# Keys of the third attention block: projected in the quantised stage before it, kept in device memory, loaded per step

## What is computed

```python
def bitlinear(x, w, b):
    xq = act_quant(rmsnorm(x))
    wq = weight_quant(w)
    return jnp.einsum('bsd,fd->bsf', xq, wq) + b
...
x = x + tanh(g_ffn[1]) * bitlinear(gelu(bitlinear(LN(x), w1, b1)), w2, b2)       # layer 1, quantised
# layer 2, masked attention; queries = LN(x), keys = values = context, 16 heads of 8
q = queries @ Wq + bq
k = keys @ Wk + bk
v = values @ Wv + bv
attn = softmax(where(masks, q k^T / sqrt(8), -1e9))
x = x + tanh(g_xattn[2]) * (rearranged(attn v) @ Wo + bo)
```

## Time and profile before

| | |
|---|---|
| median of 3 runs | 2562.04 us (2560.22 to 2562.13) |
| the profiled execution | 2556.09 us, of which its span is 2554.3 us |
| PE, DVE, ACT, POOL busy over the span | 85%, 71%, 53%, 48% |
| `l1` alone with its queue of steps | about 920 to 1190 us of the span |
| quantised stage alone | about 1190 to 1374 us |
| `l2` with its router | about 1374 to 1770 us |

### The profile page before, as it was taken

One profiled execution on the slowest core, in us unless ns is written; L12 is line 12 of the kernel. 1 busy time (PEld: TensorE's weight loads), 2 busy tenths in 40 slices (PEclk: granted clock), 3 DMA queues, 4 the chain that ended last, 5 costly groups with the idle time before them and its releaser, 6 DMA issues. The chain is left out here.

```text
span 2554.3 us, 78270 instructions
## 1 busy us (share of the span) xinstructions
PE 2168.7 (85%) x32243; PEld 1663.2 (65%) x32243; DVE 1823.6 (71%) x5057; ACT 1356.6 (53%) x2507; POOL 1213.6 (48%) x1728
## 2 busy tenths in 40 slices
PE   6999999999987959997555999993999688787597
PEld 5887887878864747775443677772566457666375
DVE  4777777777773658888985688986455388999454
ACT  3555555555542338787995555550222177788232
POOL 1334434344344531116773145556566666887444
PEclk9999999999998979998876999995999866888599
DMA  6320000000006621110000011112555322332363
GB/s 199 112 110 27 27 24 27 22 22 20 19 18 182 174 63 54 58 50 7 1 1 20 27 45 54 52 44 79 155 160 161 91 79 60 98 94 71 94 187 102
DMA packets 213955, 184.50 MB, mean 72 GB/s; under 512 B 33420, under 2 KB 189654, under 8 KB 213600
## 3 DMA queue, kind: packets, MB, share of 16 engines
q1 hardware_dynamic: 194144, 142.52, 19.2%
q0 software_dynamic: 19456, 36.99, 4.2%
HBM read 102.01 MB, written 72.68 MB: 68 GB/s over the span
## 5 line engine op out<-in xcount | busy, mean ns | idle before, releaser
L614 POOL DMA_INDIRECT slots<-row,put x256 | 258.6, 1010 | 193.1 <-issue 129.7
L1941 PE MATMUL experts_H<-experts_xs_t,experts_w 128*128 128x512 f32 x576 | 265.6, 605 | 6.9 <-DMA experts_b<-in_F_b 2.6
L1097 ACT ACTIVATE l_prob_t<-l_banks 128x512 f32<-128x512 f32 x256 | 132.2, 602 | 146.1 <-PE l_banks L1214 116.5
L1467 POOL TENSOR_TENSOR l_var_eps<-l_mv,eps 128x1 f32<-128x1 f32 x64 | 12.2, 191 | 413.9 <-DVE l_mv L1548 413.9
L1959 PE MATMUL experts_Y<-experts_w,experts_hid 128*128 128x128 f32 x1664 | 197.8, 275 | 3.5 <-DVE experts_y L1889 2.6
L1806 POOL DMA_INDIRECT rows<-experts_y,experts_idx x160 | 155.5, 972 | 91.4 <-DVE experts_y L1885 50.9
L1959 PEld LDWEIGHTS experts_Y<-experts_w,experts_hid 128*128 128x128 f32 x1664 | 191.7, 192 | 5.4 <-issue 5.4
L1503 DVE TENSOR_REDUCE l_top<-l_S 128x16 f32<-128x1024 f32 x64 | 78.3, 1224 | 160.4 <-PE l_S L1646 160.4
L1941 PEld LDWEIGHTS experts_H<-experts_xs_t,experts_w 128*128 128x128 f32 x576 | 106.1, 194 | 115.9 <-issue 107.2
L1008 DVE TENSOR_REDUCE l_top<-l_banks 128x32 f32<-128x2048 f32 x64 | 146.5, 2289 | 48.0 <-PE l_banks L1221 36.3
L912 POOL TENSOR_TENSOR l_var_eps<-l_mv,eps 128x2 f32<-128x2 f32 x96 | 24.1, 251 | 307.7 <-DVE l_mv L978 216.5
(11 more groups left out here) (312 smaller groups left out, 6041.3 us busy)
## 6 DMA issues: line engine op xcount, KB each, us to landing
experts_w<-in_F_w SPq DMA_DIRECT2D x104, 256.0 KB, 3.6
l_ctx_t<-in_ctx_t SPq DMA_DIRECT2D x96, 128.0 KB, 2.4
early_q_m<-l_q_t SPq DMA_DIRECT2D x384, 32.0 KB, 1.8
experts_xs<-slots SPq DMA_DIRECT2D x40, 264.0 KB, 2.9
slots<-l_empty SPq DMA_DIRECT2D x16, 536.0 KB, 4.0
experts_xs<-slots SPq DMA_DIRECT2D x16, 536.0 KB, 4.4
slots<-l_empty SPq DMA_DIRECT2D x16, 520.0 KB, 6.0
experts_xs<-slots SPq DMA_DIRECT2D x16, 520.0 KB, 4.4
```

The costliest lines, as they stand in the source:

```text
L614: pool.indirect_dma_start(self.slots, bass.IndirectOffsetOnAxis(ap=g.put[c][:, tile:tile + 1], axis=0), g.row[:, tile, self.sent_cols], No ...
L1097: nc.scalar.activation(prob_t[:, t.par(PROB), r, :], Z[:, r, :], ACT.Exp).then_inc(prob_done, 1)
L1941: nc.tensor.matmul(H[:, c, :], w1_s[:, t.par(2), c, :], xs_t[:, t.par(2), :], start=True, stop=True).then_inc(h_filled[c], 1)
```

## The change

The keys of `l2` for all 32 items are computed in the quantised stage, one item a step, from u = 9 to u = 40. For each, SP loads the context of the item into `ctx_t` of `l1` (step u-2 of it), TensorE does the product into a free PSUM bank, VectorE adds the bias and writes it to a slot of `k_t`, and SP stores the slot to `keys2` in device memory. The block now ends only when all stores have landed. In `l2` L1234 and L1101 are gone; SP loads the keys of an item one step before PROJ, and `k_m` is made from `k_t` in SBUF, without a bias, where it was made from PSUM. In the diff, the lines of `vector` stand between L2114 and L2123, those of `tensor` between XT and HT, SP's load of the keys behind the four DMAs of `q_m`; `l2` is called with `keys=g.keys`, the other two attentions without.

```diff
 class Quantised:
+    CTX_FIRST, KEYS_FIRST = 7, 9
...
+        self.KEYS = banks[:, 5, 0:256]
...
+    def key(self, u, first):
+        return u - first if 0 <= u - first < self.ITEMS else None
+
+    def sync(self, sp, u):
+        j = self.key(u, self.CTX_FIRST)
+        if j is not None:
+            wait(sp, self.keys_filled, j - 3)
+            sp.dma_start(self.ctx_t[:, j % 4, :], self.g.ctx_t[:, 256 * j:256 * j + 256]).then_inc(self.keys_ctx[j % 4], 16)
+        j = self.key(u, self.KEYS_FIRST)
+        if j is not None:
+            sp.wait_ge(self.keys_drained, j + 1)
+            sp.dma_start(self.g.keys[:, 256 * j:256 * j + 256], self.k_t[:, j % 4, :]).then_inc(self.keys_stored[j % 4], 16)
+        if u == self.STEPS - 1:
+            for k in range(4):
+                sp.wait_ge(self.keys_stored[k], 16 * self.ITEMS // 4)
...
 def vector(self, dve, u):
+        j = self.key(u, self.KEYS_FIRST)
+        if j is not None:
+            wait(dve, self.keys_filled, j + 1)
+            wait(dve, self.keys_stored[j % 4], 16 * (j // 4))
+            V.tensor_scalar(self.k_t[:, j % 4, :], self.KEYS, self.g.early.bk[1][:, :], None, ALU.add).then_inc(self.keys_drained, 1)
...
 def tensor(self, pe, u):
+        j = self.key(u, self.KEYS_FIRST)
+        if j is not None:
+            wait(pe, self.keys_ctx[j % 4], 16 * (j // 4 + 1))
+            wait(pe, self.keys_drained, j)
+            self.nc.tensor.matmul(self.KEYS, self.g.early.wk[1][:, :], self.ctx_t[:, j % 4, :], start=True, stop=True).then_inc(self.keys_filled, 1)
...
+                if keys is not None and t.live(3):
+                    slot = t.par(3, SLOTS_QK)
+                    wait(sp, p_filled, t.done(3 + SLOTS_QK))
+                    sp.dma_start(k_t[:, slot, :], keys[:, t.item(3) * 256:t.item(3) * 256 + 256]).then_inc(k_in[slot], 16)
...
-                    nc.scalar.activation(k_t[:, t.par(PROJ, SLOTS_QK), :], QK[:, 256:512], ACT.Identity, bias=bk_s[:, :])
+                    if keys is None:
+                        nc.scalar.activation(k_t[:, slot, :], QK[:, 256:512], ACT.Identity, bias=bk_s[:, :])
...
+                        if keys is not None:
+                            wait(act, k_in[slot], reused(t, PROJ, SLOTS_QK))
                         for j in range(4):
-                            last = nc.scalar.activation(k_m[:, t.par(PROJ, SLOTS_QK), j, :], QK[:, 256:512], ACT.Identity,
-                                                        bias=bk_masked[:, j:j + 1], scale=g.const[:, C_JMASK + j:C_JMASK + j + 1])
+                            src, bias = (QK[:, 256:512], bk_masked[:, j:j + 1]) if keys is None else (k_t[:, slot, :], 0.0)
+                            last = nc.scalar.activation(k_m[:, slot, j, :], src, ACT.Identity, bias=bias, scale=g.const[:, C_JMASK + j:C_JMASK + j + 1])
...
-                    nc.tensor.matmul(QK[:, 256:512], wk_s[:, :], ctx_t[:, t.par(PROJ, SLOTS_CTX), :], start=True, stop=True)
+                    if keys is None:
+                        nc.tensor.matmul(QK[:, 256:512], wk_s[:, :], ctx_t[:, t.par(PROJ, SLOTS_CTX), :], start=True, stop=True)
```

More of the change, by code:

```diff
@@ L773, in beats, with attention_split @@
     return max(0, min(t - first + 1, n))
-def attention_split(nc, g, name, gate_col, kind, head=None, stream=None, router=None, together=None, weights=None, out=None, follow=None):
+def attention_split(nc, g, name, gate_col, kind, head=None, stream=None, router=None, together=None, weights=None, out=None, follow=None, keys=None):
     ITEMS = TILES // 2
@@ L837, in attention_split @@
         own = len(ph.held)
-        follower = follow and follow(nc, ph, g, banks)
+        follower = follow and follow(nc, ph, g, banks, ctx_t, k_t)
+        k_in = keys is not None and [ph.sem(f"k_in{k}") for k in range(SLOTS_QK)]
         block = ctx.enter_context(nc.Block(no_gpsimd_drain=True))
@@ L891, in step @@
                     sp.dma_start(tokens(out, STREAM + 1, t), g.x[:, t.item(STREAM + 1) * 2:t.item(STREAM + 1) * 2 + 2, :]).then_inc(x_stored, 16)
-            for t in range(ITEMS + STREAM + 1):
+            for t in range(FOLLOW + follower.STEPS if follower else ITEMS + STREAM + 1):
                 if tail and t == 4:
                     tail.load(sp)
-                step(Step(sp, ITEMS, t))
+                if t < ITEMS + STREAM + 1:
+                    step(Step(sp, ITEMS, t))
+                if following(t):
+                    if t - FOLLOW == follower.CTX_FIRST:
+                        sp.wait_ge(xv_filled, XV_BEATS)
+                    follower.sync(sp, t - FOLLOW)
             if weigh:
@@ L1098, in step @@
                 if t.live(PROJ):
+                    slot = t.par(PROJ, SLOTS_QK)
                     wait(act, qk_filled, t.done(PROJ))
-                    nc.scalar.activation(k_t[:, t.par(PROJ, SLOTS_QK), :], QK[:, 256:512], ACT.Identity, bias=bk_s[:, :])
+                    if keys is None:
+                        nc.scalar.activation(k_t[:, slot, :], QK[:, 256:512], ACT.Identity, bias=bk_s[:, :])
                     last = nc.scalar.activation(q_t[:, t.par(PROJ, SLOTS_QK), :], QK[:, 0:256], ACT.Identity, bias=bq_scaled[:, :], scale=SCALE)
@@ L1342, in handed_over @@
                     pe.wait_ge(prob_done, 4 * ITEMS)
+                if u == follower.KEYS_FIRST:
+                    pe.wait_ge(xv_drained, XV_BEATS)
                 if u == follower.HT_FIRST:
@@ L1979, with __init__ @@
     STEPS = ITEMS + DEPTH - 1
-    XT_FIRST, H_FIRST, HT_FIRST, Y_FIRST = 5, 6, 10, 11
+    XT_FIRST, H_FIRST, HT_FIRST = 5, 6, 10
+    CTX_FIRST, KEYS_FIRST = 7, 9
     ROOTS, SCALES = ITEMS + 8 - 1, ITEMS + 8 - 3
-    def __init__(self, nc, ph, g, banks):
-        self.nc, self.g = nc, g
+    def __init__(self, nc, ph, g, banks, ctx_t, k_t):
+        self.nc, self.g, self.ctx_t, self.k_t = nc, g, ctx_t, k_t
+        self.keys_filled, self.keys_drained = ph.sems("keys_filled keys_drained")
+        self.keys_ctx, self.keys_stored = ([ph.sem(f"{n}{k}") for k in range(4)] for n in ("keys_ctx", "keys_stored"))
+        self.KEYS = banks[:, 5, 0:256]
         RING = self.RING
@@ L2232, in build @@
         g.slots = dram("slots2", EXPERTS * REGION, R_LOGITS - R_XN)
+        g.keys = dram("keys2", P, TOKENS)
         x0, rows2 = dram("x0", TOKENS, D), dram("rows2", 2 * TOKENS, D)
@@ L2239, in build @@
         attention_split(nc, g, "l1", 1, "softmax", stream=x0, follow=Quantised)
-        attention_split(nc, g, "l2", 2, "masked", router=(t["F2_wg"], None, "top2", g.slots), together=4, weights=6)
+        attention_split(nc, g, "l2", 2, "masked", router=(t["F2_wg"], None, "top2", g.slots), together=4, weights=6, keys=g.keys)
         experts(nc, g, "experts2", g.slots, rows2, t["F2_w1"], None, t["F2_w2"], None, "silu", 6)
```

## The result

The median goes from 2562.04 us (5 runs) to 2577.98 us (5 runs, 2567.11 to 2582.59): ratio 1.0062, 95% interval 1.0038 to 1.0087: slower, by 0.6%. The forecast was 2578. The profiled execution is the fastest of the five, 2567.11 us with a span of 2564.8, and the 10.5 us by which its span is longer than that of before have to be taken apart.

A forecast was written before the change was run, and what follows sets the result against it. In the quantised stage ScalarE was taken to bound at full clock, a ring of TensorE and VectorE waits at half clock. Profiled execution 2556.1 + 24 - 8 = 2572; the median, 6.0 higher, 2578 us; range 2556 to 2594.

The forecast's parts named there:

- The ring at half clock, ScalarE at full clock: Quantised stage: waits between TensorE and VectorE set the step at half clock (5.81 us), ScalarE at full clock (5.37 us).
- The quantised stage, +24: Keys' product and evacuation lengthen late turns by 1.17 us, 0.86 a step on the mean, 28 times: +24 us (-5 to +40).
- the count of late turns: Quantised stage: L2114 waits for Y in 19 of 26 steps, each taking all of the 1.17 us: 0.86 a step.
- The last three items and the transfers, nothing: Quantised stage: items u = 38 to 40 fit into L2114's 2.23 us wait, and loads and stores hold nothing up: 0 us.
- `l2`, -8: `l2` without L1234 saves 0.43 to 0.50 us of TensorE in each of 32 steps: -8 us, bounds 0 to -14.
- the waits of L667: `l2`, VectorE: where L667 waits, 10 times in 25 steps, L1280 comes 0.45 us earlier: 4.5 us gained, waits all but gone.
- what was named as the danger: `l2`: with less work TensorE could lose clock; half-clock time, costing 5 us today, if doubled takes 5 of the 8 back.
- the first six steps: `l2` up to 1436 us, clock 0.75: L1234 costs up to 0.84 us a step, half taken as gained: 2.6 us.
- Hidden by ScalarE: Rival, quantised stage: turns lengthen only under ScalarE's floor, step stays 5.56 us; -8, 2554 us; chance 0.09.
- half clock everywhere: Rival, quantised stage: every turn runs at half clock, +40 - 8, 2594 us; chance 0.16.
- `l2` without gain: Rival: `l2` gains nothing, since VectorE sets its steps or TensorE loses clock; +24, 2586 us; chance 0.10.
- The clock given back: Rival, quantised stage: busier TensorE gets 2.4 GHz and turns drop below 5.37 us; -5 - 8, 2549 us; chance 0.09.

The follow-up runs named there:

- after_filled: Changed kernel with four products that nobody reads added behind Y on TensorE in every full step; ratio to before 0.9959, median 2546.19 us.
- after_half_filled: Changed kernel with two products that nobody reads added behind Y on TensorE in every full step; ratio to before 0.9965, median 2545.86 us.
- transfers_only: Changed kernel without the keys' product and evacuation, storing the loaded context itself as keys, all transfers kept; ratio to before 0.9977, median 2551.31 us.
- The filled kernels: Three kernels with unread products behind Y: four on the kernel before, four or two on the changed one; ratios to before 0.9968, 0.9959, 0.9965.
- product_out: Changed kernel with the keys' product moved behind Y, the evacuation kept between L2155 and L2170, one step later; ratio to before 0.9992, median 2556.68 us.
- both_out: Changed kernel with the keys' product moved behind Y and the evacuation ahead of L2155, one step later; ratio to before 0.9977, median 2547.89 us.
- the two fills: Changed kernel with four, or with two, unread products behind Y in every full step; ratios to before 0.9959 and 0.9965.

## Why the prediction was right

That forecast and median, 2578 and 2577.98, agree this closely is luck: the five executions spread over 15 us, and the profiled one, which the sum put at 2572, took 2567.11. What was right are the path and the signs of the two terms; their sizes came out as follows.

*The ring at half clock, ScalarE at full clock: right.* The changed kernel lengthens the turn and not ScalarE's work, and ScalarE's idle time went from 4.9 to 30.2 us, above the 25 named. That full clock would hide the new work was an argument when it was written; after_filled and after_half_filled show it, 5.33 and 5.34 us.

*The quantised stage, +24: measured +27.0 (bounds -5 to +40).* The product was put at 0.84 us at half clock and took 0.85; the evacuation at 0.33 and took 0.39. The term was too small in the count of late turns: 19 of 26 were taken over from before, and 24 of 26 waited. Most late turns were cheaper than thought, 6.74 us (1231.79 - 1225.05) and not 6.98 (three took 7.35), since H still runs at 2.4 GHz in a turn like the one shown: 0.62 us, where the turn of before had 1.01; only XT, the product and HT behind it have 1.2. The two errors stand against each other: 1.04 us a step against 0.86. That count did not fit the step of before either: 19/26 x 5.81 + 7/26 x 5.37 = 5.69, where 5.56 had been measured, since a turn that is not late can take 4.98 us (1255.59 - 1250.61). The 26 full steps, 26 x 1.04, make up all of the +27.0: the stretch ahead of them, with the first items, took 0.4 us more than before, the one behind them 0.4 less.

*The last three items and the transfers, nothing: right.* From the last L2170 to the last L2176 it is 18.31 us, against 18.70 from L2123 to L2129. The last evacuation starts 5.2 us before that last L2176, and its store has landed by 1393.1. In transfers_only the same stretch takes 21.46 us, but not for its transfers: its last three HT take 1.97 us each, at 1.2 GHz, where the last two of before took 1.10 and 1.09.

*`l2`, -8: measured -8.0, and -7.1 over all kernels* (the mean of the eight with loaded keys is 320.0 us, of the four without 327.0). The step of the argument that put it at the waits of L667 was wrong: they are not all but gone, 4.1 us are left of 5.8. The gain is a whole product, 0.43 us, in each short step, and what was named as the danger, clock that is lost in `l2` as well, took a part back: the steady part went from 0.98 to 0.95. That the sum still came to 8 is luck too. The sixth queries' product of `l2`, before and after:

```profile
1428.26 0.59 PE L1235 MATMUL l_banks<-l_xn_t,early_wq 128*128 128x256 f32 x2
```

```profile
1444.97 0.67 PE L1251 MATMUL l_banks<-l_xn_t,early_wq 128*128 128x256 f32 x2
```

Up to it `l2` gained 54.85 - 48.83 = 6.0 us, where 2.6 had been put on the first six steps; behind it 273.65 - 271.65 = 2.0 us, where 4.5 + 0.8 had been put on the waits of L667 and L1035. Over all kernels, eight against four as above, the two parts are 3.8 and 3.3 us.

*The rivals.* Hidden by ScalarE, half clock everywhere and `l2` without gain fall by the rows above. The clock given back did not come, 0.73 after 0.75, and the reason named against it is borne out: the gap in which TensorE waits for VectorE stayed, and it grew from 58.9/26 = 2.3 us to 2.6. The Trainium skill (TensorE: Matmul & The Clock Gate, Part 1) has it that activity releases the throttle. The filled kernels agree with that, at 0.99 to 1.00; the changed kernel, with one product more in each step, stayed at 0.73, but its step grew with the work, and TensorE's busy share only went from 84.32/145 = 58% to 103.93/172 = 60%. The share alone does not tell the clock either: it is 66% in product_out at 0.79 and 66% in after_half_filled at 1.00. What went with the clock was where the work stands: both_out does the same work as the changed kernel at 0.88.

## What to carry to other kernels

Work that is added to an engine with idle time need not be free. Here it was free outside the ring of waits that sets the step, and inside it only once the ring, at full clock or opened, had become shorter than ScalarE's step: look for the wait that the engine ends its idle time with, and put the work into it, not ahead of it. Where a stage runs at both clock levels, price an added product at each, and look at whether the edit closes or stretches TensorE's gap, since the clock can be worth more than the work. A second place in PSUM that takes H's wait for its reading out altogether gave the lowest ratio here, 0.9940, with all of the change's other edits kept; the two fills gave 0.9959 and 0.9965, with intervals that overlap it.

## What the hardware showed that we had not expected

Two products of 128 x 256 f32 that nobody reads, 1.08 us in a step of 5.34, brought TensorE's clock from 0.73 to 1.00 and the whole kernel from 1.0062 to 0.9965 of before. H's wait became 0.8 us shorter by it; whether the shorter wait or the added work brought the clock up no run separates.

In `l2` the clock fell in steps in which TensorE hardly paused: 12.51 of 12.69 us busy at a clock of 0.73. What stands ahead of the slow part in that step of the changed kernel:

```profile
1494.12 2.05 PE L1287 MATMUL l_banks<-l_val,l_prob_t 128*64 128x18 f32 x64
1496.35 0.28 PE L1338 MATMUL l_banks<-early_bias_rows,const_bf 3*128 3x128 bf16 x2 [0.18 <-DVE l_top L1019]
1496.56 1.13 PE L1343 MATMUL l_banks<-early_wo,l_ctx_out 64*64 64x128 f32 x16
```

L1343 takes 1.13 us here and 0.67 in a step at full clock:

```profile
1560.80 0.28 PE L1338 MATMUL l_banks<-early_bias_rows,const_bf 3*128 3x128 bf16 x2 [0.19 <-DVE l_top L1019]
1561.02 0.67 PE L1343 MATMUL l_banks<-early_wo,l_ctx_out 64*64 64x128 f32 x16
```

Ahead of it are 64 narrow products and one pause of 0.18 us. The step with 0.67 has the same order, with a pause of 0.19, and no fall; what the fall goes by stays open.
